# Graph network on Trainium2: neighbour sums by three bf16 matmuls on exactly split rows instead of one fp32 matmul

## What is computed

```python
x = _layernorm(x + _L0_gnn_ref(x, src, dst, ...))      # sum of x[src] * norm by dst, then two linear maps with gelu
x = _layernorm(x + _L1_gnn_ref(x, ..., edge_type_8))   # attention over the edges of a node, one head, 8 relations
x = _layernorm(x + _L2_gnn_ref(x, src, dst, ...))      # sum of x[src] by dst, then two linear maps with relu
x = _layernorm(x + _L3_gnn_ref(x, edge_attr_64, ...))  # attention with 4 heads and edge features
```

```python
msg = x[edge_src] * norm[:, None]
agg = jax.ops.segment_sum(msg, edge_dst, num_segments=N)
...
neigh = jax.ops.segment_sum(feat[src], dst, num_segments=N_NODES)
```

## Time and profile before

| what | value |
|---|---|
| median of three runs | 11083.2 us (11058.91 to 11108.54) |
| span of the profiled execution | 11064.0 us |
| the profiled execution's own time | not given apart from its span |
| PE matmuls, busy | 3739.3 us, 34% |
| PE weight loads, busy | 3432.3 us, 31% |
| VectorE, busy | 3269.5 us, 30% |
| ScalarE, busy | 228.8 us, 2% |
| GpSimd, busy | 6323.3 us, 57% |
| granted TensorE clock, mean | 0.50 of full speed |

### The profile page before, as it was taken

One profiled execution on the slowest core, in us unless ns is written; L12 is line 12 of the kernel. 1 busy time (PEld: TensorE's weight loads), 2 busy tenths in 40 slices (PEclk: granted clock), 3 DMA queues, 4 the chain that ended last, 5 costly groups with the idle time before them and its releaser, 6 DMA issues. The chain is left out here.

```text
span 11064.0 us, 65181 instructions
## 1 busy us (share of the span) xinstructions
PE 3739.3 (34%) x16686; PEld 3432.3 (31%) x16691; DVE 3269.5 (30%) x3857; ACT 228.8 (2%) x792; POOL 6323.3 (57%) x6584
## 2 busy tenths in 40 slices
PE   7333333335222233333323332333412222233333
PEld 6333333334222232332323332333412212223223
DVE  7100101004211121221224454544522222332323
ACT  0000000002000000000000000000000000000000
POOL 6666666665554455655366666666454444555552
PEclk5555555555555555555555555555555555555555
DMA  3311111112111111111111111111121111111110
GB/s 56 61 23 23 23 23 23 23 23 87 23 19 18 18 20 22 22 20 22 27 42 47 48 48 47 49 49 45 34 44 20 20 19 22 22 25 25 24 25 18
DMA packets 334682, 345.48 MB, mean 31 GB/s; under 512 B 183228, under 2 KB 212360, under 8 KB 327850
## 3 DMA queue, kind: packets, MB, share of 16 engines
q0 software_dynamic: 209952, 220.30, 11.6%
q1 hardware_dynamic: 124676, 124.51, 3.9%
HBM read 304.50 MB, written 40.68 MB: 31 GB/s over the span
## 5 line engine op out<-in xcount | busy, mean ns | idle before, releaser
L1175 POOL DMA_INDIRECT rows_a<-table,idx_c_a x1612 | 1536.9, 953 | 1405.7 <-ACT idx_c_a L1142 924.1
L1175 POOL DMA_INDIRECT rows<-table,idx_c_a x1612 | 1544.7, 958 | 1188.5 <-ACT idx_c_a L1142 706.7
L701 PE MATMUL acc_a<-msg_a,hot_a 128*128 x6640 | 1614.6, 422 | 1414.3 <-issue 1224.9
L938 POOL DMA_INDIRECT rows_l<-table,idx_c_l x1612 | 1524.9, 946 | 900.4 <-issue 493.1
L701 PEld LDWEIGHTS acc_a<-msg_a,hot_a 128*128 128x128 f32 x6640 | 1486.8, 327 | 1527.3 <-issue 1520.2
L938 POOL DMA_INDIRECT rows<-table,idx_c_l x1548 | 1463.4, 945 | 834.5 <-issue 468.4
L967 DVE TENSOR_TENSOR hot_l<-side_l,neg_tl 128x2048 f32<-128x2048 f32 x208 | 472.0, 2283 | 3140.0 <-remote 2864.3
L701 PE MATMUL acc_l<-rows_l,hot_l 128*128 x3320 | 779.5, 388 | 1578.5 <-issue 1466.5
L701 PEld LDWEIGHTS acc_l<-rows_l,hot_l 128*128 128x128 f32 x3320 | 770.1, 322 | 1588.6 <-issue 1588.0
L701 PE MATMUL acc_l<-rows,hot_l 128*128 x3320 | 783.2, 390 | 1404.9 <-issue 1313.7
L701 PEld LDWEIGHTS acc_l<-rows,hot_l 128*128 128x128 f32 x3320 | 768.4, 322 | 1420.4 <-issue 1419.8
(11 more groups left out here) (298 smaller groups left out, 2541.8 us busy)
## 6 DMA issues: line engine op xcount, KB each, us to landing
feat<-edge_attr SPq DMA_DIRECT2D x50, 1031.2 KB
rows<-table,idx_c_a POOLq DMA_INDIRECT x1612
rows_l<-table,idx_c_l POOLq DMA_INDIRECT x1612
rows_a<-table,idx_c_a POOLq DMA_INDIRECT x1612
rows<-table,idx_c_l POOLq DMA_INDIRECT x1548
table<-stage SPq DMA_DIRECT2D x49, 260.0 KB
spread<-zero SPq DMA_DIRECT2D x12, 832.0 KB
hot_a<-spread SPq DMA_DIRECT2D x2, 3328.0 KB
```

What stands on the lines that cost most here:

```text
L701: return nc.tensor.matmul(acc[:, bass.ds(at, row.shape[-1])], hot, row, start=False, stop=True, skip_group_check=True)
L938: pool.indirect_dma_start(rows[:, half * BODY + s * CH + k, 0:D], None, table, bass.IndirectOffsetOnAxis(idx_c[:, s, k:k + 1], 0))\
L1175: pool.indirect_dma_start(rows[:, u, k, 0:row], None, table, bass.IndirectOffsetOnAxis(idx_c[:, u, k:k + 1], 0)).then_inc(gathered[u], 16)
```

## The change

Each gathered row is split into three bf16 parts whose sum is the fp32 value: the high half of its bits, the high half of what is left, and the rest. ScalarE takes the high halves (L913 of the changed kernel) and those of the remainder (L915), VectorE forms the remainder (L989) and the last part (L991). The parts go to a ring `packs` of 128 tiles x 3 x 65 bf16 values; the ring of fp32 rows shrinks to 64 tiles. The one-hots are bf16. A visit is three matmuls, one per part, into the same columns. The waits are for constants: `copied`, `split` and `hot_ready`. The tables `lands` and `frees` and what makes them go; what attention needs of `offs` becomes a table of its own, `needs`. Some buffers share the room of `packs` in layer 0, and for that the parts of the first 64 tiles wait until all are scaled (`scaled`). The list of chunk c + 4 is copied after the parts of chunk c.

```diff
-                rows = rows0 if early else tsb(f"rows_{tag}", [P, RING, D + 1])
+                rows = rows0 if early else tsb(f"rows_{tag}", [P, BODY, D + 1])
+                packs = packs0 if early else tsb(f"packs_{tag}", [P, RING, PARTS3, PW], BF16)[:]
+                rest = tsb(f"rest_{tag}", [P, CH, PW])
+                rows_v = rows[:].rearrange("p t f -> p (t f)")
+                high_of_rows = rows_v.bitcast(BF16).rearrange("p (t f n) -> p t f n", f=PW, n=2)[:, :, :, 1]
+                high_of_rest = rest[:].rearrange("p t f -> p (t f)").bitcast(BF16).rearrange("p (t f n) -> p t f n", f=PW, n=2)[:, :, :, 1]
-                hot = tsb(f"hot_{tag}", [P, BODY, P])
+                hot = tsb(f"hot_{tag}", [P, BODY, P], BF16)
...
                     def _(act):
-                        def tiles(c, s, n):
-
+                        def lists(c, s, n):
+                            nc.scalar.copy(idx_c[:, s, 0:n], src_tt[:, bass.ds(c * CH, n)]).then_inc(chunk_ready, 1)
+
+                        def parts(i, s, half, n, ahead):
+
+                            c = i * SLOTS + s
+                            if isinstance(c, int) and c < fetched:
+                                act.wait_ge(scaled, 1)
+                            else:
+                                act.wait_ge(gathered[s], i * (16 * CH) + 16 * n)
                             if not (isinstance(c, int) and c < 2 * SLOTS):
-                                freed = nc.values_load(frees[0:1, bass.ds(c - 2 * SLOTS + 1, 1)], engines=ACT_ONLY, min_val=2, max_val=1 + VCHUNKS,
-                                                       skip_runtime_bounds_check_because=BOUNDED)
-                                act.wait_ge(summed, freed)
-                            if not (isinstance(c, int) and c < fetched + SLOTS):
-                                act.wait_ge(gathered[s], (c - s) * (16 * CH // SLOTS))
-                            nc.scalar.copy(idx_c[:, s, 0:n], src_tt[:, bass.ds(c * CH, n)]).then_inc(chunk_ready, 1)
+                                act.wait_ge(summed, c - 3)
+                            to = packs[:, half * BODY + s * CH:half * BODY + s * CH + n]
+                            nc.scalar.copy(to[:, :, 0], high_of_rows[:, s * CH:s * CH + n]).then_inc(copied, 1)
+                            act.wait_ge(rest_ready, c + 1)
+                            nc.scalar.copy(to[:, :, 1], high_of_rest[:, 0:n]).then_inc(copied, 1)
+                            if ahead:
+                                act.wait_ge(copied, 2 * c + 1)
+                                lists(c + SLOTS, s, ahead)
...
                             for k in range(n):
-                                pool.indirect_dma_start(rows[:, half * BODY + s * CH + k, 0:D], None, table, bass.IndirectOffsetOnAxis(idx_c[:, s, k:k + 1], 0))\
+                                pool.indirect_dma_start(rows[:, s * CH + k, 0:D], None, table, bass.IndirectOffsetOnAxis(idx_c[:, s, k:k + 1], 0))\
...
+                        def parts(i, s, half, n):
+
+                            c = i * SLOTS + s
+                            if not (isinstance(c, int) and c < fetched):
+                                dve.wait_ge(gathered[s], i * (16 * CH) + 16 * n)
+                            if not (isinstance(c, int) and c == 0):
+                                dve.wait_ge(copied, 2 * c)
+                                dve.wait_ge(split, c)
+                            here = slice(s * CH, s * CH + n)
+                            nc.vector.tensor_tensor(rest[:, 0:n], rows[:, here], high_of_rows[:, here], ALU.subtract).then_inc(rest_ready, 1)
+                            dve.wait_ge(rest_ready, c + 1)
+                            nc.vector.tensor_tensor(packs[:, half * BODY + s * CH:half * BODY + s * CH + n, 2], rest[:, 0:n], high_of_rest[:, 0:n], ALU.subtract)\
+                                .then_inc(split, 1)
...
+                        def add_parts(at, k, place):
+
+                            for n in range(PARTS3):
+                                last = nc.tensor.matmul(acc[:, bass.ds(at, PW)], hot[:, k], places[:, bass.ds(place + n * PW, PW)],
+                                                        start=False, stop=True, skip_group_check=True)
+                            return last
...
-                                if first:
-                                    for m in range(s + 1):
-                                        pe.wait_ge(gathered[m], 16 * CH)
-                                else:
-                                    _, landed = nc.values_load_multi_w_load_instructions(
-                                        lands[0:1, bass.ds(c, 1)].rearrange("o c n -> o (c n)"), engines=PE_ONLY, min_val=16 * CH, max_val=16 * CH * CHUNKS,
-                                        skip_runtime_bounds_check_because=BOUNDED)
-                                    for m in range(SLOTS):
-                                        pe.wait_ge(one, 1)
-                                        pe.wait_ge(gathered[m], landed[m])
-                                size = end if s == SLOTS - 1 else CH
+                                tiles = min(c + 1, CHUNKS) if isinstance(c, int) else c + 1
+                                pe.wait_ge(copied, 2 * tiles)
+                                pe.wait_ge(split, tiles)
                                 pe.wait_ge(hot_ready, c + 1)
-                                for k in range(size):
-                                    ins = add_visit(acc, at[k], hot[:, s * CH + k], places[:, bass.ds(place[k], D + 1)])
+                                for k in range(end if s == SLOTS - 1 else CH):
+                                    ins = add_parts(at[k], s * CH + k, place[k])
```

More of the change, by code:

```diff
@@ L28 @@
 I32 = mybir.dt.int32
+U16 = mybir.dt.uint16
 ALU = mybir.AluOpType
@@ L78 @@
 AW = 68
+PARTS3 = 3
+PW = D + 1
+PLACE = PARTS3 * PW
 BANK = 512
@@ L880, in gather_sum @@
                 gathered = early_in if early else [sem(f"gathered_{tag}_{s}") for s in range(SLOTS)]
-                rates = early(tsb, rows, acc) if early else None
+                scaled = sem(f"scaled_{tag}")
+                rates = early(tsb, rows, acc, scaled) if early else None
                 hot_ready = sem(f"hot_ready_{tag}")
+                copied = sem(f"copied_{tag}")
+                rest_ready = sem(f"rest_ready_{tag}")
+                split = sem(f"split_{tag}")
                 summed = sem(f"summed_{tag}")
@@ L915, in _ @@
-                        for c in range(fetched, 2 * SLOTS):
-                            tiles(c, c % SLOTS, CH)
-                        with act.Fori(2, CHUNKS // SLOTS) as i:
-                            for s in range(SLOTS):
-                                tiles(i * SLOTS + s, s, CH)
-                        tiles(CHUNKS - 1, (CHUNKS - 1) % SLOTS, REST_T)
+                        def lists(c, s, n):
+                            nc.scalar.copy(idx_c[:, s, 0:n], src_tt[:, bass.ds(c * CH, n)]).then_inc(chunk_ready, 1)
@@ new lines, in turn @@
+                        def turn(i, half):
+                            for s in range(SLOTS):
+                                parts(i, s, half, CH, CH)
+                        for c in range(fetched, SLOTS):
+                            lists(c, c, CH)
+                        turn(0, 0)
+                        turn(1, 1)
+                        with act.Fori(1, ITERS // 2 - 1) as j:
+                            turn(2 * j, 0)
+                            turn(2 * j + 1, 1)
+                        for s in range(SLOTS):
+                            parts(ITERS - 2, s, 0, CH, 0 if s else REST_T)
@@ L1056, in attend @@
                 tsb, tps = fresh(nc, st)
[L1057 to L1060 removed]
+                rows = tsb(f"rows_{tag}", [P, 2, S, width])
                 idx_c = tsb(f"idx_c_{tag}", [P, 2, S], I32)
```

148 lines of the change are left out of this document (66 added, 82 removed).

## The result

The changed kernel takes **11,754.7 us** (median of 4 runs, 11,752.3 to 11,761.4) against 11,085.8 us for the kernel before on the same chip: 1.061 times as long, 95% interval 1.058 to 1.064. 11,690 was predicted, in a range of 10,930 to 11,930.

A forecast was written before the change was run, and what follows sets the result against it. The prediction took items per us, not work, as the bound of both plain sums; +343, +266 and -3 us gave +606 on a span of 11,064, and with 19 us outside it 11,690 us, range 10,930 to 11,930.

The forecast's parts named there:

- (a): Both plain sums: nine items a visit instead of five, 6640 more items a sum; +249 and +251 us.
- the faster rival: Plain sums: bf16 visits free the ring early and GpSimd's issue becomes the bound; total 10,700 us; chance 0.17.
- The price by one cycle: Other pricing of (a): 22 visits instead of 40 while GpSimd issues, the rest in its standstill; +300 to +500 us.
- (b): Both plain sums: two more ScalarE copies and two VectorE operations per chunk, 404 items; +15 us a sum.
- (d): Plain sums: GpSimd transfers slowed beside VectorE operations with two SBUF inputs; taken as zero, up to 200 us in all.
- The third rival: Plain sums: the chain of copy, subtract, copy holds, not the count; 260 us, total 11,400 us; chance 0.15.
- The sign that it named: The third rival's sign: a PE that waits for `split` rather than for issue.
- (c): First plain sum: tiles 64 to 127 can start only after the rates, so 64 tiles come into the stage; +79 us.
- (e): Tables `lands` and `frees` and setup operations go: -3 us; the new constant waits zero, with 270 us as other end.
- (f): Attention stages: `needs` loaded apart, one load a group more or less; zero.
- GpSimd as the bound: Another name for the faster rival: GpSimd's issue bounds both plain sums; total 10,700 us; chance 0.17.
- Pace by visits: Plain sums: the slow stretch lets through as many visits as before, whatever their items; about 11,110 us; chance 0.10.

The follow-up runs named there:

- e5: e1 with two more pairs of a load and a one-column bf16 zero matmul per visit in both plain sums; 1.048 of the kernel before.
- e8: Changed kernel without the subtractions and the middle part's copy, all three matmuls of a visit reading the high part; 1.039 of the kernel before.
- e10: e8 with one matmul of the high part per visit instead of three; 1.019 of the kernel before.
- e9: e1 with the lists for tiles 64 to 127 of layer 0's sum copied only after the rates; 1.023 of the kernel before.
- e1: Kernel before with constant waits instead of lands and frees, and needs and start as U16; rows stay fp32; 1.025 of the kernel before.
- e6: Changed kernel with the U16 table needs loaded twice per eight visits in both attention stages; 1.112 of the kernel before.
- e12: e9 with messages and one-hots in bf16 in both attention stages; 0.967 of the kernel before, 10,728 us against 11,101.
- e2: e1 with four empty instructions ahead of each plain-sum visit, which did not reach the program; 1.025 of the kernel before.
- e4: Changed kernel with attention's needs as I32 again, each value raised to at least zero in a register; 1.061 of the kernel before.

## Why the prediction was right, and where it wasn't

The sign, the range and the holder were right. In the slow stretch the PE gets its instructions through at a pace that doesn't depend on what they do (2.8 us from one single matmul to the next, in fp32, in bf16 and with one column), nine a visit instead of five cost time, and GpSimd stands longer, 13.5 us after 48 tiles. The size was luck: +606 came out near +669 by errors that cancelled. The two sums with the stretches behind them were priced at 343 and 266 us and took 248 and 205 more; attention, priced at zero, took 188 more, and setup 47 more instead of 3 less. The loop of the first sum ended at 2744 us, not near 2850. Term by term:

- **(a), 6640 more items a sum at 26.7 per us: +500 in all.** Measured 258 (e5, with the pairs' own time in it) and 229 (e8 less e10). The mechanism holds, the term was mis-sized by two. The step that failed is the division by one common rate: it takes a packet of the software queue and an instruction of the PE for equal. By the count of the prediction the changed kernel shows 67,564 items in 2479.8 us, 27.2 per us, e5 28.0 and e10 25.5, where the rate should have been one. Nor do the two stages agree so well if the hardware queue's packets are counted, which the sum left out, 9287 in the first and 14,214 in the second: 31.0 and 32.6 per us. The degree count's 32.5 per us, which I wrote down as the strongest row against me, had said so; I gave it to the faster rival instead of correcting the weights.
- **The price by one cycle** (+300 to +500 for (a)) started from "the PE gets through the same number of items while GpSimd issues". Its lower end was nearer than the count, and its standstill of 14 to 17 us near the 13.5 measured.
- **(b), the splits' items: +30.** With (d) and the chain of copy, subtract, copy it was 0.013 of the ratio (changed kernel less e5), 145 us give or take 60; e8 gives some 110 beside the items. The third rival had 260 for the chain alone; its price was too high, but it wasn't nothing. The sign that it named is weak: in layer 0's sum the PE waited 60 us for VectorE's last part and 1615 us for issue.
- **(c), tiles 64 to 127 behind the rates: +79.** Measured -14 (e9). The step that failed is that work hidden beside other work is won: by the same count that I used for the sums, the transfers had taken the rates' instructions their share, 114 us against 47.
- **(d), GpSimd beside two-input operations: zero, 200 at most.** 10 to 13 ns a transfer, about 36 us of its time in both sums.
- **(e), tables and waits: -3.** Layer 0's sum is 32 us longer with the constant waits (e1), layer 2's isn't. Setup was to shrink by 3 us; it was 47 longer in the profiled execution. The trace shows a slow stretch inside it. A stretch of the degree count, before:

```profile
100.00:150.00 50.00, 37.14 (x346) 32.19 (x345) 35.17 (x37) 7.55 (x6) 41.91 (x27) 0.50 0.45 20
```

and after:

```profile
100.00:150.00 50.00, 17.20 (x123) 12.28 (x120) 11.21 (x18) 7.56 (x6) 38.97 (x37) 0.64 0.38 25
```

  A third of the matmuls, and more transfers of GpSimd. It goes with the execution and not with the kernel: up to there e6 has the instructions of the changed kernel, and its last matmul of the degree count ends at 236 us against 292; e12 has those of e9, and ends at 305 against 239. Of the 14 traces, before, e2, e4, e6 and e9 end the count at 236 to 255 us, the others at 283 to 305. So the 47 us aren't shown to be the change's. What tips it wasn't tried.
- **(f), attention: zero.** +188 with the stretches behind it. The step that failed: "one load a group more or less" counted loads and didn't ask how long one of another type takes. The trace of before had no U16 load; it should have been bounded, not set to zero. How much of the 188 us the U16 loads explain stays open (e4, e6).

Of the rivals, GpSimd as the bound is out: even three items a visit leave the second sum 265 us above its pace (e10). Pace by visits is out by e8 and e10, which have the same number of visits and lie 229 us apart. The two sentences of the Trainium skill (page NOTIFIC — the notification-queue block, sections Interfaces and Constraints, capacities, measured rates) can be weighed now. The zero cost of a record is given there beside a rate of at least 6.6 million records a second. The prediction counted 26.7 items per us, so if the items are records, this case lies above that rate and doesn't refute the sentence; each cost 0.017 to 0.019 us. That the block can stall an engine fits, but no run here shows that it is this block. One rival stays open with it: span and clock were recorded for every run here, the timed ones too, so no run tells whether the same pace holds when nothing is recorded.

## What to carry to other kernels

Where single cheap instructions on several engines stand evenly spaced while a gather queue runs, count instructions before work: splitting one matmul into three cheaper ones lowers the PE's busy time and lengthens the kernel. Price an item by adding some that do nothing useful, not by dividing the span by a sum of unlike things, and read in the timeline what they take when nothing holds them, or their own time passes for the price of the count. Before a difference in a stage is put down to an edit, look at a run that has the same instructions there. And look at what a hidden transfer does to the work that hides it, and at the load of every table whose type an edit changes.

## What wasn't expected of the hardware

- A register load of eight U16 values takes 1925 ns, of eight I32 values 590 ns.
- A packet of the software queue seems to weigh about two instructions: at 0.0194 us an item (258 / 13,280), layer 2's 2312 us before hold 119,200 items; less 9800 instructions and transfers and shared among 51,520 packets, that is 2.1 for each; at the 0.017 us of e8 and e10 it would be 2.4. This is an estimate from these runs and the earlier trace rows, and takes the whole sum to be paced by items. It would also let the degree count's rate pass (2.1 x 12.2 + 20.4 = 46 per us, under 52). No run varied the packets.
- The granted clock was 1.00 through layer 0's sum in e1 and 0.50 in e2, which is in effect the same program, and the stage took 2278 and 2276 us.
- The same instructions of setup took 236 us in one execution and 292 in another (e6 and the changed kernel), up to the end of the degree count.
